# Attention kernel on eight cores: the projection tile handed over in four pieces instead of two

## The reference, cut to what matters

```python
# x: (4, 4096, 1024), 16 heads of 64
h = layernorm(x) * ln_gamma + ln_beta
q, k, v = split(h @ w_qkv + b_qkv)            # per head
scores = einsum('bhqd,bhkd->bhqk', q, k) / 8
out = einsum('bhqk,bhkd->bhqd', softmax(scores), v)
x = layernorm(x + (x + out @ w_out + b_out))
s = x @ Win + bin_                            # then a small block-diagonal FFN
x = layernorm(x + (x + ffn(s)))
```

## Time and profile before

| what | value |
|---|---|
| time, median of 3 runs | 2196.34 us (2195.33 to 2234.6) |
| the profiled execution's own time | 2198.03 us |
| its span, slowest core (core 6) | 2196.5 us (all cores 2186.4 to 2196.5) |
| busy: PE, ACT, DVE | 1474.7 us (67%), 1359.4 us (62%), 608.1 us (28%) |
| mean granted TensorE clock, core 6 | 0.857 of full |

### The profile page before, as it was taken

One profiled execution on the slowest core, in us unless ns is written; L12 is line 12 of the kernel. 1 busy time (PEld: TensorE's weight loads), 2 busy tenths in 40 slices (PEclk: granted clock), 3 DMA queues, 4 the chain that ended last, 5 costly groups with the idle time before them and its releaser, 6 DMA issues. The chain is left out here.

```text
span 2196.5 us, 26829 instructions; the slowest of 8 cores (2186.4 to 2196.5 us)
## 1 busy us (share of the span) xinstructions
PE 1474.7 (67%) x8552; PEld 513.1 (23%) x8552; DVE 608.1 (28%) x806; ACT 1359.4 (62%) x1478; POOL 26.1 (1%) x35
## 2 busy tenths in 40 slices
PE   0443388868877886788688778868885775454443
PEld 0221122222322222222223222222221222122111
DVE  2333311231222123222312221232223001246555
ACT  3677277757776776777577767766675887031212
POOL 0000000000000000000000000000000000000000
PEclk9776589989998999999899989998998999676565
DMA  6222000000010001000100100010000000502111
GB/s 103 83 80 68 0 1 6 6 5 6 1 10 1 6 1 11 1 5 1 10 5 2 11 1 6 1 10 1 6 1 1 1 1 2 115 9 77 42 35 77
DMA packets 44598, 44.36 MB, mean 20 GB/s; under 512 B 34993, under 2 KB 35122, under 8 KB 44466
## 3 DMA queue, kind: packets, MB, share of 16 engines
q1 hardware_dynamic: 16162, 33.72, 5.2%
q0 software_dynamic: 28304, 8.92, 4.1%
HBM read 43.16 MB, written 8.39 MB: 23 GB/s over the span
## 5 line engine op out<-in xcount | busy, mean ns | idle before, releaser
L816 ACT ACTIVATE PT_sb<-score_ps,negB_sb 128x1024 bf16<-128x1024 f32 x1024 | 1140.2, 1114 | 365.8 <-PE score_ps L751 158.2
L749 PE MATMUL score_ps<-qT_sb,kT_sb 64*128 64x512 bf16 x1024 | 405.7, 405 | 209.9 <-ACT PT_sb L816 117.5
L765 PE MATMUL pv_ps<-PT_sb,v_sb 128*64 128x512 bf16 x1024 | 405.1, 396 | 15.8 <-ACT PT_sb L816 13.7
L751 PE MATMUL score_ps<-qT_sb,kT_sb 64*128 64x512 bf16 x1024 | 410.1, 410 | 0.0
L769 PE MATMUL pv_ps<-PT_sb,v_sb 128*64 128x512 bf16 x1024 | 406.5, 397 | 0.0
L775 PE MATMUL z_ps<-PT_sb,onesb_sb 128*64 128x512 bf16 x1024 | 393.8, 385 | 0.0
L772 PE MATMUL z_ps<-PT_sb,onesb_sb 128*64 128x512 bf16 x1024 | 393.0, 384 | 0.0
L604 PE MATMUL qkv_ps<-xhq_sb,wq_sb 128*128 128x512 bf16 x1120 | 326.8, 419 | 53.9 <-DVE qT_sb L619 27.1
L749 PEld LDWEIGHTS score_ps<-qT_sb,kT_sb 64*128 64x128 bf16 x1024 | 92.8, 94 | 596.1 <-issue 596.1
L826 DVE RECIPROCAL zb_sb<-z_ps 128x512 f32<-128x512 f32 x32 | 107.4, 3358 | 290.7 <-PE z_ps L775 254.2
L765 PEld LDWEIGHTS pv_ps<-PT_sb,v_sb 128*64 128x64 bf16 x1024 | 112.0, 109 | 198.4 <-issue 148.4
(11 more groups left out here) (80 smaller groups left out, 831.3 us busy)
## 6 DMA issues: line engine op xcount, KB each, us to landing
xtile_sb<-x SPq DMA_DIRECT2D x32, 512.0 KB, 4.4
xres_sb<-x SPq DMA_DIRECT2D x16, 512.0 KB, 8.4
out<-u_sb SPq DMA_DIRECT2D x16, 512.0 KB, 3.7
wq_sb<-wqkv POOLq DMA_DIRECT2D x24, 256.0 KB, 5.5
wout_sb<-wout POOLq DMA_DIRECT2D x1, 2048.0 KB, 22.3
win_sb<-win POOLq DMA_DIRECT2D x1, 128.0 KB, 22.5
rw_sb<-rw POOLq DMA_DIRECT2D x1, 128.0 KB, 22.6
w2b_sb<-w2b POOLq DMA_DIRECT2D x1, 128.0 KB, 22.6
```

The source lines that it names most:

```text
L749: e.matmul(o, w, r, start=True, stop=True))
L751: e.matmul(o, w, r, start=True, stop=True).then_inc(st.h, 1))
L765: a=s0, b=s1: e.matmul(o, w, r, start=a, stop=b, skip_group_check=True))
L816: e.activation(out=o, in_=i_, func=AF.Exp, bias=b, scale=0.125))
```

## The change

In `qkv_steps_gen` the generator now also yields before matmul 2 and before matmul 6 of a projection tile. A tile has 5 steps instead of 3: four of two matmuls each, and the bias. No instruction is added or removed, only the slots that instructions fall into. The number of slots stays 72, and the generator's steps go from 73 to 113.

```diff
             for kc in range(8):
-                if kc == 4:
+                if kc in (2, 4, 6):
                     yield (m, n, "mid")
                 last = kc == 7
```

## The result

The changed kernel takes 2370 us (median of 9 runs, 2367 to 2388), the kernel before 2193 to 2196 us. The ratio is 1.0805 with a 95% interval of 1.0776 to 1.0833: slower by 8%. The forecast was 2386 us and a range of 2335 to 2425, and its ratio to 2196 was 1.086. The profiled execution took 2367.7 us, its span is 2366.2 us on core 5, and the cores lie between 2358.5 and 2366.2 us. (Some runs of some kernels, of the kernel before too, are longer, as one die has a lower granted clock in them; the ratios are made without the longest of these.)

What follows compares the result with a forecast made beforehand. In the attention stage neither ACT nor TensorE was taken to bound alone. A subgroup becomes 175.4 + 54.5 = 229.9 us against 202.8, 27.1 us more, 7 times, 190 us: 2386 us, range 2335 to 2425.

Steps and rivals of the forecast that it cites:

- The count of slots and steps: Generator per subgroup: 113 steps for 72 slots, so 41 steps are left behind the fourth pass.
- The passes: Four attention passes of a subgroup with the gaps between them: 175.4 us to the fourth pass's last exponential.
- The run: Leftover generator work behind the fourth pass, where ACT has nothing to do: 54.5 us, 7 times.
- The stall: First part of the run, from the fourth pass's last exponential to the transposes: 6.7 us.
- the bound: Three blocks of squares, matmuls and maxima in the run, at half clock: 25.9 us.
- the small operations: End of the run, from the bound to the next subgroup's first exponential: 2.1 us.
- transposes and five tiles: In the run: 0.5 us, then 23.5 us at half clock, less 4.2 us for half the tiles at full clock.
- Half and full clock throughout: Two rivals, the run wholly at one clock: half gives 2417 us, chance 0.27; full gives 2338 us, chance 0.13.
- The passes at the floor: Rival: smaller pieces also remove stalls at pass ends, four passes of 38.5 us: 2276 us, chance 0.06.
- The short run: Rival: tiles overlap their bias, the run is as short as its PE work, 17 us: 2126 us, chance 0.02.
- The sign in the profile: ACT's idle time before the exponential (L816) should grow from 366 us to about 555 us.
- The other signs: Profile after: gaps some 54 us, passes 39 to 42 us, tiles 3 to 4.6 us and bound matmuls 1.86 us apart.

Runs made afterwards that it cites:

- the ballast: Changed kernel plus matmuls nobody reads, 14 in the stall behind the fourth pass and 4 behind each bound matmul in the run: 2347 us, ratio 1.068.
- e7: Changed kernel, but tiles that start in the run behind the fourth pass alternate between the one bank and half the score buffer: 2338 us, ratio 1.0658.

## Why the prediction held

**The count of slots and steps** (113 against 72, 41 left) was right, and it is the cause: the kernel with pieces of four and fewer slots reproduces the loss, the one with three and a half tiles fewer in the run has the run of 43.5 us that the rows give for it, and the one with five steps a tile, no run and the bound at even key tiles is back at 2193 us.

**The passes.** Predicted 175.4 us up to the fourth pass's last exponential, measured 227.2 - 52.3 = 174.9 us. The four passes, put at 40.0, 39.0, 40.0 and 42.2 us, were 39.6, 39.3, 39.7 and 42.1 on the mean of seven, the gaps of 2.8, 8.6 and 2.8 us were 2.8, 8.5 and 2.8.

**The run.** Predicted 54.5 us, measured 52.3 us on the mean of seven. The stall was 6.7 us as taken from the earlier trace rows, the bound 25.6 us for the 25.9 taken from the earlier trace rows, the small operations 2.2 for 2.1. The step that was off is that of the tiles: transposes and five tiles, half of them at full clock, were 0.5 + 23.5 - 4.2 = 19.8 us, and the rows show 475.66 - 457.59 = 18.1 us. Two tiles ran through a change of the clock (2.99 and 3.30 us of matmuls), three at full, and those took 2.97 us. Taking half of the tiles at full clock was a choice between two readings, not a result of either; that the clock rose where it did, so that the sum is off by so little, is luck. This, some tenths in the bound and 0.5 us in the passes make the 2.7 us a subgroup, 19 us in all, by which the forecast was over: 7 x 24.4 = 171 us came, 190 were predicted.

**Half and full clock throughout.** Both fell as whole cases: the clock was half, then full, then half in one run. What the ballast adds is that forcing the clock up is worth 22 us, less than the 79 us between the two cases.

**The passes at the floor.** They came to 38.8 and 39.6 us, which is near the 38.5, but the stalls at pass ends stayed, as DVE's order had it.

**The short run.** Its mechanism, that tiles overlap their bias, was built in e7 and is worth 32 us, far from the 260 by which the rival lay under the forecast. Why it could not win: half of the run is the bound, in which every matmul waits for the maximum before it.

**The sign in the profile** that was named first was wrong: the idle time before L816 fell, since ACT's wait for the run ends at L707. The sum of both grew by 170 us. The other signs (gaps of some 54 us, passes of 39 to 42 us, tiles 3 to 4.6 us apart, bound matmuls 1.86 us apart) were there.

**Smaller slips.** ACT's 365.8 us before L816 were not mostly a wait for a score: 158.2 us were, and 136.6 us were a wait for the products (L775), as ACT's waits in the section on the result show. The rivals' times lack the 1.7 us that the forecast takes off for the profiled execution, which changes none of them.

**What the prediction did not say.** It had no price for a bound step inside a pass, as it needed none. The first expectations took that price from the kernel before, where every second key tile has no step, and missed by 130 and 208 us. The kernels with a slot at every key tile show that this price grows at consecutive key tiles, by the spacing itself and by the half clock that came with it.

## What to carry to other kernels

Where a generator feeds work into slots, count steps against slots before making pieces smaller: what does not fit comes out in one piece where nothing covers it, and here it held two chains (tile, bias, tile; matmul, maximum, matmul) that run at the pace of two engines' turns. Put a wait for another engine ahead of the instruction that needs it, not behind the one that caused it; in this kernel that one line was worth 62 us, some 58 of them in the attention stage. After that the slots should go by kind, so that nothing stands behind a long operation of the engine that it waits for.

## What was not expected of the hardware

A bound step holds PE for nearly the same time at even key tiles and at consecutive ones (from its matmul to PE's next instruction 1.5 to 1.9 us in the fourth passes of the kernel before, 1.7 to 2.0 us with one at each key tile), but ACT was idle for it for 0.7 to 1.1 us with a free key tile beside it, for 1.4 to 1.8 us at consecutive ones at full clock, and for 2.0 to 3.2 us at consecutive ones at half clock. And the granted clock came back to full inside the run: it rose while transposes and a tile's matmuls ran behind one another for the second time, and stayed at 1.00 through three tiles with waits of 1.1 us between them, while in the opening stage the two tiles at 231.63 and 236.19, also parted by a wait, stayed at half.
